# The additions ahead of three norms' roots move from VectorE to GpSimd in a graph-attention and mixture-of-experts block

## The reference

```python
x = x + gnn(layernorm(x), adj)      # 4 heads of attention over the neighbours
x = x + ffn(layernorm(x))

def layernorm(x):                   # over the 128 channels
    return (x - mean(x)) / sqrt(var(x) + 1e-5)

def ffn(x):
    h = rmsnorm(x) * ln1            # rmsnorm: x * rsqrt(mean(x * x) + 1e-6)
    x = x + attention(h) @ wo.T     # 4 heads, causal, with rope
    flat = rmsnorm(x) * ln2
    w = top2(softmax(flat @ router.T))          # 8 experts, 2 for each token
    return x + sum_e w[e] * ((silu(flat @ w1[e].T) * (flat @ w3[e].T)) @ w2[e].T)
```

## Time and profile before

| | |
|---|---|
| median of 3 runs | 1731.81 us (1727.41 to 1735.3) |
| the profiled execution | 1738.94 us, span 1737.1 us |
| TensorE busy | 1524.0 us (88% of the span) |
| VectorE busy | 1409.4 us (81%), 4725 instructions |
| ScalarE busy | 1052.2 us (61%) |
| GpSimd busy | 913.5 us (53%), 720 instructions |
| scatter-adds `out<-ys,xt` (L452) | 264, 430.5 us busy on GpSimd |
| routing DMAs `routed<-fx,slot` (L436) | 256, 257.9 us busy on GpSimd |

### The profile page before, as it was taken

How to read it: one execution, slowest core, us unless ns; L and a number is a source line. 1 busy time by engine, 2 the same in 40 slices (tenths; PEclk the granted TensorE clock), 3 DMA queues, 4 the chain that set the end, 5 groups by cost and what they waited for, 6 DMA issues and landing times. The chain is left out here.

```text
span 1737.1 us, 40737 instructions
## 1 busy us (share of the span) xinstructions
PE 1524.0 (88%) x10930; PEld 1122.8 (65%) x10930; DVE 1409.4 (81%) x4725; ACT 1052.2 (61%) x4092; POOL 913.5 (53%) x720
## 2 busy tenths in 40 slices
PE   4778998999899899999999999999999899987672
PEld 3555666776676667766667676777676666765451
DVE  4678888898889888988898888888889888875441
ACT  3576666766666667666666666666666666653221
POOL 2134565555555555556656655556555555555433
PEclk8899999999999999999999999999999999999897
DMA  5001222222222222222222222222222222222221
GB/s 153 9 27 45 42 37 44 48 47 48 50 41 50 36 46 48 47 48 50 41 51 41 41 49 47 48 48 50 47 45 40 42 47 47 41 43 44 42 33 20
DMA packets 141737, 79.08 MB, mean 46 GB/s; under 512 B 31909, under 2 KB 137165, under 8 KB 141261
## 3 DMA queue, kind: packets, MB, share of 16 engines
q0 software_dynamic: 46208, 34.37, 14.3%
q1 hardware_dynamic: 94349, 41.90, 9.8%
q10 hardware_dynamic: 960, 0.20, 0.1%
HBM read 33.16 MB, written 43.26 MB: 44 GB/s over the span
## 5 line engine op out<-in xcount | busy, mean ns | idle before, releaser
L452 POOL DMA_INDIRECT out<-ys,xt x264 | 430.5, 1631 | 511.5 <-DMA out<-ys,xt 383.4
L436 POOL DMA_INDIRECT routed<-fx,slot x256 | 257.9, 1007 | 199.1 <-DVE slot L845 131.7
L1132 PE MATMUL bank<-w_s,hsT 128*128 (+1 forms) x1584 | 230.3, 282 | 17.2 <-ACT hsT L599 16.5
L1132 PEld LDWEIGHTS bank<-w_s,hsT 128*128 128x128 f32 (+1 forms) x1584 | 202.8, 192 | 65.7 <-issue 60.9
L592 ACT ACTIVATE sg<-bank 128x341 f32<-128x341 f32 x264 | 120.6, 457 | 165.0 <-PE bank L1111 149.3
L541 ACT ACTIVATE p<-ub,nm 128x128 f32<-128x128 f32 x512 | 198.0, 390 | 34.3 <-DVE nm L767 33.7
L1111 PE MATMUL bank<-w_s,xT 128*128 x528 | 203.0, 466 | 6.6 <-DVE xT L907 3.0
L598 ACT ACTIVATE hsT<-bank 128x256 f32<-128x256 f32 x264 | 101.2, 384 | 165.7 <-PE bank L1125 141.1
L913 DVE SCALAR_TENSOR_TENSOR hg<-sg,bank 128x341 f32<-128x341 f32 x264 | 133.7, 507 | 82.8 <-ACT sg L592 77.1
L1115 PE MATMUL bank<-w_s,xT 128*128 x528 | 197.0, 455 | 0.1
L1125 PE MATMUL bank<-ident,hu 128*128 128x128 f32 (+1 forms) x792 | 137.6, 283 | 54.1 <-DVE ys L931 43.0
(11 more groups left out here) (165 smaller groups left out, 3372.9 us busy)
## 6 DMA issues: line engine op xcount, KB each, us to landing
xt<-routed SPq DMA_DIRECT2D x264, 65.0 KB
xs<-in_x SPq DMA_DIRECT2D x32, 256.0 KB
out<-bs SPq DMA_DIRECT2D x32, 256.0 KB
out<-ys,xt POOLq DMA_INDIRECT x264
routed<-fx,slot POOLq DMA_INDIRECT x256
w_s<-in_w SPq DMA_DIRECT2D x2, 1364.0 KB
adj<-in_adj SPq DMA_DIRECT2D x32, 64.0 KB, 2.9
w_s<-in_w SPq DMA_DIRECT2D x2, 512.0 KB
```

The source lines that it names most:

```text
L436: pool.indirect_dma_start(routed, bass.IndirectOffsetOnAxis(slot[p][:, i:i + 1], 0), fx[i // GB][p][:, i % GB, :], None).then_inc(S[f"sc{p ...
L452: pool.indirect_dma_start(out_rows, bass.IndirectOffsetOnAxis(xt[r][:, C:C + 1].bitcast(I32), 0), ys[r][:], None, compute_op=ALU.add, **bo ...
L1132: last = pe.matmul(y_p[:, 0:C], hsT[r % 2][0:n, c, :], w2_s[0:n, bass.ds(e, 1), c, :].rearrange("p a c -> p (a c)"), start=c == 0, stop=c ...
```

## The change

In all three places the addition (and the scaling, where there is one) is taken out of VectorE's program and written into GpSimd's, right ahead of the root. GpSimd now waits for the statistics (`mv_g`, `mv_a`) or for ScalarE's sum (`sq`) where it waited for VectorE's result, and after the addition it waits for its own result by the same semaphore as before. The tables of order are as they were; VectorE has no function for `ms` any more.

```diff
 # GpSimd, nx
                     if late(n, 1):
                         pool.wait_ge(S["xn"], 4 * n)
+                    pool.wait_ge(S["mv_g"], 4 * n + 4)
+                    pool.tensor_scalar(ve_g[:], mv_g[:, :, 1], EPS_LN, None, ALU.add).then_inc(S["ve_g"], 1)
                     pool.wait_ge(S["ve_g"], n + 1)
                     pool.tensor_tensor(rstd[:], ve_g[:], half[:, 0, :], ALU.pow).then_inc(S["rstd"], 1)
 # GpSimd, na
-                    pool.wait_ge(S["va"], a + 1)
+                    pool.wait_ge(S["mv_a"], 4 * a + 4)
                     if late(a, 1):
                         pool.wait_ge(S["hN"], 4 * a)
+                    v = mv_a[:, :, 1]
+                    pool.tensor_scalar(va[:, 0, :], v, EPS_LN, None, ALU.add)
+                    pool.tensor_scalar(va[:, 1, :], v, 1.0 + EPS_RMS, EPS_RMS * EPS_LN, ALU.mult, ALU.add).then_inc(S["va"], 1)
+                    pool.wait_ge(S["va"], a + 1)
                     pool.tensor_tensor(rr[:], va[:], half[:], ALU.pow).then_inc(S["norm_a"], 1)
 # GpSimd, ms
+                    pool.wait_ge(S["sq"], t + 1)
+                    pool.tensor_scalar(ve_t[:], ms[:], 1.0 / C, EPS_RMS, ALU.mult, ALU.add).then_inc(S["ve_t"], 1)
                     pool.wait_ge(S["ve_t"], t + 1)
                     pool.tensor_tensor(r3[:], ve_t[:], half[:, 0, :], ALU.pow).then_inc(S["r3"], 1)
 # VectorE, nx
-                    dve.wait_ge(S["mv_g"], 4 * n + 4)
-                    dve.tensor_scalar(ve_g[:], mv_g[:, :, 1], EPS_LN, None, ALU.add).then_inc(S["ve_g"], 1)
 # VectorE, na
-                    dve.wait_ge(S["mv_a"], 4 * a + 4)
-                    v = mv_a[:, :, 1]
-                    dve.tensor_scalar(va[:, 0, :], v, EPS_LN, None, ALU.add)
-                    dve.tensor_scalar(va[:, 1, :], v, 1.0 + EPS_RMS, EPS_RMS * EPS_LN, ALU.mult, ALU.add).then_inc(S["va"], 1)
 # VectorE
-                def ms_():
-                    dve.wait_ge(S["sq"], t + 1)
-                    if late(t, 1):
-                        dve.wait_ge(S["r3"], t)
-                    dve.tensor_scalar(ve_t[:], ms[:], 1.0 / C, EPS_RMS, ALU.mult, ALU.add).then_inc(S["ve_t"], 1)
```

More of the change, by code:

```diff
@@ L931, in weigh @@
                         dve.tensor_scalar(ys[r][:], y_p[:, 0:C], xt[r][:, C + 1:C + 2], None, ALU.mult).then_inc(S["ys"], 1)
-                return {"nx": nx, "na": na, "xn": xn_, "hN": hN_, "wo": wo_, "ms": ms_, "f": f_, "q": q_, "kk": kk_, "lg": route1,
+                return {"nx": nx, "na": na, "xn": xn_, "hN": hN_, "wo": wo_, "f": f_, "q": q_, "kk": kk_, "lg": route1,
                         "rank": route2, "tab": tab, "p1": scores1, "s2": max2, "ot": ot, "rb": rb, "yT": yT_, "x": out_x, "u": gate, "g": gated, "d": weigh}
```

## The result

The changed kernel takes 1770.6 us (median of 6, 1765.2 to 1776.8) against 1731.6 us (median of 6, 1727.4 to 1735.3) for the kernel before. The ratio is 1.022, 95% interval 1.0193 to 1.0248: 38 us slower, where 25 were forecast.

What follows compares the result with a forecast made beforehand. It took a loop with GpSimd in each link as the bound. Four instructions and three waits add 0.97 us a round; 26 rounds give 25.2 us on a median of 1731.8, so 1757 us, range 1738 to 1778.

Steps and rivals of the forecast that it cites:

- The bound: Whole round of 48.3 us: GpSimd is in each link of the pace-setting loop, so its added time is paid; chance 0.66.
- the forecast's 7 us: From `r3` to `slot`: the 0.26 us added ahead of `r3` delays `bs`, `fx` and `slot` each round.
- The size of the added time: GpSimd ahead of the roots: four instructions of 0.19 us and three waits of 0.07 us, 0.97 us a round.
- The waits and gaps: GpSimd ahead of each root: three waits a round for its own result, 0.07 us each, upper end 0.15.
- VectorE's gain at nothing: VectorE's four removed instructions: 10 to 22 us over 32 rounds, counted at nothing as VectorE waits for `rr` and `r3`.
- The hold by `bs`: Behind `r3`: `bs` on GpSimd seems to hold VectorE, the four `fx` finishing some 0.7 us after it.
- The first rival: From `slot` to `r3`: VectorE's time counts, GpSimd's does not; 10 to 22 us back, 1716 us; chance 0.08.
- The second rival: Landings between `rr` and `r3`, or TensorE's pace, swallow the delay: about 1735 us, no change; chance 0.16.
- The third rival: GpSimd's small instructions are dear: 2.25 us a round, 58 us, 1790 us; chance 0.10.
- The signs named for it: Profile after: GpSimd rows 0.15 to 0.25 us, links about 17.0 and 14.8 us, `rr` wait near 1.1, rounds 50.3.

Runs made afterwards that it cites:

- e1: Kernel before with only the sum ahead of the root `rstd` moved from VectorE to GpSimd: 1748.2 us, ratio 1.0048.
- e2: Kernel before with only the two sums for `va`, ahead of the root `rr`, moved from VectorE to GpSimd: 1761.0 us, ratio 1.0119.
- e3: Kernel before with only the sum ahead of the root `r3` moved from VectorE to GpSimd: 1741.2 us, ratio 1.0005.
- e11: e3 with three more such sums into scratch ahead of `r3`, each with a wait for itself: 1790.7 us, ratio 1.0284 against the kernel before.
- e4: Kernel before with VectorE's four instructions taken out and put nowhere, constants and 1/C left out: 1735.2 us, ratio 0.9957.
- e5: Kernel before, VectorE keeping its sums, plus four like sums on GpSimd into scratch and a wait for itself ahead of each root: 1774.9 us, ratio 1.0215.
- e10: Kernel before with GpSimd's sum `bs` moved from behind `r3` to behind the scatter-add of tile 0: 1715.1 us, ratio 0.9862.
- e7: Kernel before with GpSimd's root `r3` and sum `bs` ahead of the scatter-add of tile 7 in place of behind it: 1710.4 us, ratio 0.9845.

## Why the prediction was right, and where it was off

- **The bound.** "GpSimd is in each link" of the loop held for the links from `slot` to `rr`: e1 and e2 pay in full, and C grew by 1.10 us. For the link from `r3` to `slot` the forecast's 7 us did not show: e3, late by 0.31 us, is as fast as the kernel before. A further delay there is paid in full at full clock (e11, 0.86 us for 0.82). Where e3's 0.31 us went is not settled: a small slack and a gain of VectorE by the missing `ve_t` would both give it (e4's 7.5 us, not divided by place, would be enough), and no run took them apart.
- **The size of the added time.** The term that was mis-sized is the instruction. I took 0.19 us from the mask; measured were 0.26, 0.32, 0.195 and 0.20 us, 0.975 in place of 0.76 us a round. The waits and gaps cost 0.33 us (1.30 less 0.975) in place of 0.21. With 1.30 in place of 0.97 the same sum gives 26 x 1.30 = 34 us, and 1766 us. That this comes so near the measured 38 is in part luck: 8 of the 34 us belong to the place that cost nothing by itself (e3), and about as much shows only with all three together. Some 3 us of that are rounds with the lowered clock; the rest is not explained.
- **VectorE's gain at nothing.** Alone it is 7.5 us (e4), so it was not nothing; beside the late roots e5 leaves it open. The rule written for it, that the cover is the wait for `rr` and the change makes it longer, is what the waits show: `hN` waits 53.9 us in place of 10.6.
- **The hold by `bs`.** Read from 0.7 us between two ends, it is shown by e10.
- **The first rival** (faster by 16 us) needed VectorE's waits to be chance. e4 gives it 7.5 us at most, and only without the additions.
- **The second rival** (swallowed) may be true in part: D is 0.58 us a round shorter in the profile of the change, but about 0.3 us of that is in e1, e2 and e3 too, whatever place they move, and e3's delay cost nothing. It did not reach the other two places.
- **The third rival** (dear) did not come: the added time is 1.30 us a round, a third over the forecast and far from its 2.25. A way to a dear outcome that was not among its reasons is what a late `r3` does to TensorE's clock; it cost some 3 us here, and far more in e11.
- **The signs named for it.** New rows of 0.15 to 0.25 us: two of the four lie above. From the first routing DMA to `rr`'s root some 17.0 us forecast: 17.26 in the round shown (942.67 to 959.93). From the sum ahead of `r3` to the first routing DMA 14.8 us forecast: 14.27 (977.58 to 991.85), but that sum starts only when the scatter-add ahead is through, 0.6 us later than `r3` did. The wait for `rr` near 1.1 us a round: 1.67. Rounds of 50.3 us: 50.23.

## What to carry to other kernels

An engine busy half of its time can be the one that sets the pace: look for where it is the last to arrive (an instruction of another engine that starts 0.04 us behind it, round after round) before giving it work, and price small instructions by start-up, not by size (0.20 to 0.32 us for four columns). Time saved on an engine that waits for the same result is worth little: here 7.5 us of the 10 to 22 taken away, with nothing added elsewhere. If a result is late because its engine waits in program order for something unrelated (here a landing), moving the instruction one place up is worth more than any instruction saved: e7 gains 27 us with one word moved, and it makes the whole change three times cheaper.

## What the hardware showed that I had not expected

- A `tensor_scalar` of 128x4 on GpSimd takes 0.20 us right behind another small sum or once the scatter-add ahead is through, and 0.26 to 0.32 us behind the mask and a routing DMA, while one of 128x512 (bytes in, bf16 out) takes 0.62 us: 128 times the columns in two to three times the time.
- A sum on GpSimd with two operands in SBUF slows a `tensor_scalar` or a copy of VectorE beside it. `fx` takes 1.66 us in the mean beside `bs` and 0.87 us without. VectorE's copy into `riE` got faster in the change, where `x1` on GpSimd comes behind it (it starts 1.03 us later in the round shown), while before the two ran side by side; the groups of before and after:

```profile
L794 DVE COPY riE<-ri_ 128x512 f32<-128x512 f32 x32 | 37.9, 1184 | 1.1
```

```profile
L790 DVE COPY riE<-ri_ 128x512 f32<-128x512 f32 x32 | 18.1, 565 | 1.1
```

  That is 20 us of busy time saved that the waits take back: `st_a`, which waits for `x1`, now waits 46.1 us in place of 3.9. It hangs on where the two meet and not on the change as such: the same copy takes 1.52 us in the mean in e1 and e5.
- Behind one hold of VectorE, with TensorE busy 0.93 of 4 us, the granted clock fell to 0.50, and the step from `r3` to the first routing DMA got 2.9 us longer; in the other rounds of e11 and of the change with a lowered clock 1.4 to 2.9 us. By the medians a delay ahead of `r3` cost nothing for 0.3 us and 49 us for 1.1 us: the part above the loop's 22 us comes in the rounds in which the clock fell.
